# A chain of eight image layers: where GpSimd takes a norm's power in the first two stages

## The reference

```python
x = x + gate_conv(ln(x))       # stage 0: softmax gate over the 256 pixels
t = t + topk_ffn(ln(t))        # stage 1: FFN for the 127 best of 256 tokens of each image
x = x + deform_conv(ln(x))     # stage 2: deformable 3x3
t = t + moe_gelu(ln(t))        # stage 3: 8 experts
x = x + attention(ln(x))       # stage 4
t = t + moe_64(ln(t))          # stage 5: 8 experts
x = x + spectral_conv(ln(x))   # stage 6: 3x3 conv with weights w / sigma
t = t + moe_ln(ln(t))          # stage 7: 8 experts

def ln(v):                     # in every stage
    return (v - mean(v)) / sqrt(var(v) + eps)

def sigma(w, a, b, c):         # depends on the weights alone, complex numbers
    for _ in range(20):
        d = normalize(einsum('oihw,o,i,h->w', w, a*, b*, c*))
        c = normalize(einsum('oihw,o,i,w->h', w, a*, b*, d*))
        b = normalize(einsum('oihw,o,h,w->i', w, a*, c*, d*))
        a = normalize(einsum('oihw,i,h,w->o', w, b*, c*, d*))
    d = normalize(...)
    return abs(einsum('oihw,o,i,h,w->', w, a*, b*, c*, d*))
```

## Time and profile before

| | |
|---|---|
| median of 3 runs | 1166.83 us (1162.14, 1166.83, 1176.15) |
| the profiled execution | 1172.36 us, of which the span of instructions is 1170.6 us |
| mean granted TensorE clock in it | 0.850 of full speed |
| busy in the span | TensorE 81%, VectorE 60%, ScalarE 42%, GpSimd 38% |
| stage 0, stage 1 in the profile | about 27 to 135 us, about 138 to 240 us |

### The profile page before, as it was taken

How to read it: one execution, slowest core, us unless ns; L and a number is a source line. 1 busy time by engine, 2 the same in 40 slices (tenths; PEclk the granted TensorE clock), 3 DMA queues, 4 the chain that set the end, 5 groups by cost and what they waited for, 6 DMA issues and landing times.

```text
span 1170.6 us, 16680 instructions
## 1 busy us (share of the span) xinstructions
PE 951.9 (81%) x4266; PEld 567.0 (48%) x4266; DVE 697.0 (60%) x2439; ACT 493.2 (42%) x966; POOL 445.8 (38%) x1234
## 2 busy tenths in 40 slices
PE   2656387758998998989888777799988767999998
PEld 2545265435554555555534434465554554444443
DVE  2876676746455664554467756656675554566653
ACT  1322222245445654552445445333343012666664
POOL 4565566631543535446244221134564321111100
PEclk9999996659889988998789887857779666999999
DMA  4500000000000000000000000000000000000000
GB/s 74 86 0 1 0 1 0 0 1 1 1 1 0 0 0 0 1 1 1 1 0 1 0 0 1 1 0 0 0 1 0 1 0 0 5 5 4 9 5 9
DMA packets 26352, 6.21 MB, mean 5 GB/s; under 512 B 24068, under 2 KB 26244, under 8 KB 26308
## 3 DMA queue, kind: packets, MB, share of 16 engines
q1 hardware_dynamic: 26308, 5.70, 2.8%
HBM read 4.65 MB, written 1.05 MB: 5 GB/s over the span
## 4 chain that ended last, share of the span: by engine, by line
PE 44%; issue 16%; DVE 10%; POOL 5%; ACT 4%; DVEq 0%; POOLq 0%; ACTq 0%; another core or an unknown queue 0%
PE banks L1449 8%; PE banks L1275 6%; PE banks L1158 5%; PE banks L1159 3%; PE banks L1089 3%; PE banks L1466 2%; PE banks L1473 2%; PE banks L1267 2%; PE banks L1417 2%; DVE weighted L1994 1%; DVE summed L1998 1%; DVE V L1720 1%; PE banks L1263 1%; PE banks L1230 1%; POOL rstd L646 1%
## 5 line engine op out<-in xcount | busy, mean ns | idle before, releaser
L962 ACT ACTIVATE scratch<-banks,b 128x512 f32<-128x512 f32 x224 | 144.3, 683 | 57.2 <-PE banks L1159 45.1
L1449 PE MATMUL banks<-scratch,W 128*64 128x512 f32 (+1 forms) x448 | 151.8, 661 | 0.4
L1889 DVE TENSOR_TENSOR scratch<-banks,XR 128x1024 f32<-128x1024 f32 x72 | 87.5, 1224 | 87.3 <-PE banks L1267 61.1
L1158 PE MATMUL banks<-VS,W_hi 128*128 128x512 f32 x240 | 120.6, 503 | 2.1 <-DVE X L2067 1.0
L646 POOL TENSOR_TENSOR rstd<-vareps,neghalf 128x4 f32<-128x4 f32 x64 | 66.8, 1044 | 128.6 <-DVE vareps L1708 124.0
L1159 PE MATMUL banks<-VS,W_lo 128*128 128x512 f32 x240 | 106.4, 443 | 0.0
L1994 DVE SCALAR_TENSOR_TENSOR weighted<-banks,b,cwide 128x512 f32<-128x512 f32 x72 | 53.9, 748 | 73.7 <-PE banks L1449 72.9
L1275 PE MATMUL banks<-scratch,region 128*64 128x256 f32 x576 | 88.0, 432 | 3.0 <-DVE scratch L1889 3.0
L1720 DVE TENSOR_SCALAR V<-X,moments,rstd 128x64 f32 (+1 forms) x256 | 67.6, 328 | 36.7 <-POOL rstd L646 32.6
L973 ACT ACTIVATE cwide<-banks 128x512 f32<-128x512 f32 x96 | 57.4, 598 | 73.8 <-PE banks L1466 73.5
L1132 PE MATMUL banks<-ident,V 128*128 128x128 f32 x128 | 33.7, 354 | 58.5 <-DVE V L1720 58.4
(11 more groups left out here) (289 smaller groups left out, 2039.6 us busy)
## 6 DMA issues: line engine op xcount, KB each, us to landing
W<-in_L_ffn_W SPq DMA_DIRECT2D x3, 512.0 KB
X<-in_x SPq DMA_DIRECT2D x8, 128.0 KB, 2.7
out<-X SPq DMA_DIRECT2D x8, 128.0 KB, 2.0
cwide<-in_L_ffn_W SPq DMA_DIRECT2D x2, 256.0 KB
KC<-in_L_conv_kernel SPq DMA_DIRECT2D x2, 144.0 KB
W<-in_L_ffn_W SPq DMA_DIRECT2D x1, 256.0 KB
cwide<-in_L_ffn_w SPq DMA_DIRECT2D x2, 128.0 KB
Ko<-in_L_conv_w SPq DMA_DIRECT2D x1, 144.0 KB, 3.7
```

Source lines behind the costliest of these rows:

```text
L962: act.activation(hid[:, c % 4, :], bank[c % 2][:, :], ACT.Gelu, bias=b1[s][:, w:w + 1]).then_inc(h_ready, 1)
L1158: pe.matmul(out, hi, VS[u][:], start=True, stop=False)
L1449: ins = pe.matmul(y, W2[s][:, w, :], hid[:, c % 4, :], start=opens, stop=closes, skip_group_check=True)
L1889: vec.tensor_tensor(S[:, k % 3], pair(p), xr, ALU.mult).then_inc(s_ready, 1)
```

## The change

In `body`, which sets GpSimd's order, `seg1` now stands ahead of the norm's power (`prep`) in stages 0 and 1 too, as it did in stage 2. In stage 5 it stays where it was.

```diff
--- before.py
+++ after.py
@@ -662,7 +662,7 @@
                     step = None if s not in STEP0 else i * 2 + (STEP0[s] + u) if s == 2 else i + STEP0[s]
                     first_half = step is not None and (u == 0 or s == 2)
                     second_half = step is not None and (u == 1 or s == 2)
-                    if s == 2:
+                    if s == 2 or first_half and s < 2:
                         seg1(step)
                     if s in MOE and (u == 0 or not wrap):
                         powers(i * 2 + (MOE0[s] + u + 1), s)
@@ -670,7 +670,7 @@
                         prep(i * 2 + 2 - wrap, s_next)
                     elif not wrap:
                         prep(i * 2 + 3, s)
-                    if s != 2 and first_half:
+                    if s > 2 and first_half:
                         seg1(step)
                     if first_half:
                         seg2(step)
```

## The result

| | before | changed |
|---|---|---|
| median of 20 runs each | 1166.71 us | 1158.83 us |
| lowest to highest | 1158.55 to 1176.15 | 1151.97 to 1167.97 |
| profiled execution, span | 1170.6 us | 1164.1 us |
| mean granted TensorE clock in it | 0.850 | 0.847 |

The ratio, which leaves out runs over 1.5% above the fastest of their kernel, is 0.9936, 95% interval 0.9916 to 0.9956: 0.64% less time, 7.5 us (the two medians lie 7.9 us apart). The 20 runs of one kernel spread over 16 to 18 us, so the total alone says that the change helps, but not through what. The traces say that, since kernels with the same code up to a mark reach it at nearly the same time: stage 1 starts at 134.38 and 134.35 us in two kernels with the old order in stage 0, at 130.16, 130.18 and 130.55 in three with the new one.

The account below looks back on a forecast made before the run. It took a closed loop with GpSimd's power as a link to bound stage 0's and 1's trips; 0.5 + 3.0 + 0 + 3.3 + 0.4 = 7.2 us off the 1166.83 median gives 1159.6 us, range 1153 to 1167.

Parts of the forecast that it names:

- The closed loop: Stage 0's second trip: GpSimd, TensorE and VectorE wait for each other in a loop of 25.04 us, GpSimd's power being one link.
- Stage 0, trips two to four: `seg1` starts 1.01 us earlier per trip, where the power stood, covered by TensorE's 3.63 us idle: 3.0 us in all.
- The first trip: Stage 0: `T1` is ready at 35.79, so `seg1` starts at about 35.9 instead of 36.41, 0.5 us gained.
- Stage 1's first trip: TensorE is busy turning the block's output until 148.68, later than `bsq` at 148.00, so gain and price are both 0.
- Stage 1, trips two to four: The power's distance to `seg1` comes off each trip, covered by TensorE's idle time: 1.15 + 1.15 + 1.0 = 3.3 us.
- The 0.4 us for a faster `seg1`: Stage 1: VectorE stands still during part of `seg1`, which then runs 0.13 us faster a trip, 0.4 us in all.
- TensorE's cover in stage 1: TensorE's idle time of 1.56 us before `slot2` covers the earlier `seg1`, leaving 0.4 us.
- The sign of right and wrong: Profile sign at line 1108: TensorE's idle time in stage 1 would be 0.4 us instead of 1.56.
- The thin cover: Stage 1: with the power behind `seg1`, V is ready only 0.2 to 0.3 us before TensorE turns it.
- The late norm: Rival: TensorE waits for V in stage 1 instead, losing half that stage's gain, 1.7 us: 1161.3 us, chance 0.13.
- The later stages: Stages 2 to 7: nothing behind stage 1 changes its order, so they shift as they are.
- rivals of a better and a colder clock: TensorE's mean clock 0.01 higher, 1153.6 us, chance 0.13; or lower in stages 2 to 7, about 1166 to 1172, chance 0.12.

## Why the prediction was right

The forecast was 1159.6 us and 0.6% less; measured were 1158.83 and 0.64%. The mechanism was right; that the sum came out so near is in part luck, as two errors cancel. Its steps one by one:

**The closed loop** was right. GpSimd, TensorE and VectorE wait for each other in a ring, so a microsecond in it is a microsecond of the trip, although GpSimd is busy 38% of the span and has 5% of the chain. A second power cost 4.3 us in stage 0 ahead of `seg1` and 0.4 behind it, and taking the one behind away gave nothing more.

**Stage 0, trips two to four**, was sized 3.0 us and gave 4.22 - 0.64 = 3.58. The excess is 0.15 to 0.2 us a trip. `seg1` itself runs in 2.10 instead of 2.17 us; the rest is spread over several distances of 0.01 to 0.04 us. **The first trip**, bounded by `T1`, was sized 0.5 and gave 0.64.

**Stage 1's first trip**: forecast 0, measured -4.18 against -4.22, so 0.

**Stage 1, trips two to four**, was sized 3.3 us, with 0.4 us more for a faster `seg1`, and gave 6.94 - 4.18 = 2.76. **The 0.4 us for a faster `seg1`** had the wrong sign: it became slower by 0.08 to 0.17 us a trip. This is the one term that failed, and it explains most of what is missing: 0.4 us that did not come and 0.35 that were lost. The loops shrank by 25.86 - 24.83 and 25.83 - 24.80, that is 1.03 us each, where 1.15 + 0.13 was forecast. The excess of stage 0 (0.7 us with its first trip) and the lack of stage 1 (0.9 us) cancel, so the sum is better than its parts.

**TensorE's cover in stage 1** was read too simply. The prediction took the idle time of 1.56 us for a fixed cover and expected 0.4 us to be left. In the changed kernel it is 2.48, 2.63 and 0.76 us in the three trips, by the level of TensorE's clock. Where the matmuls were slow, 0.52 us was left, so the sum of the prediction is right for that level. The sign of right and wrong that it derived from it was not one.

**The thin cover** was right in size: 0.2 to 0.3 us forecast, 0.33 measured. The late norm took nothing. It begins at once behind that: a second power makes TensorE wait 0.75 us. The norm of line 1720 was expected to wait for `rstd` in eight places. VectorE idles in front of it in seven: in stage 0's first trip it comes just after the power's end (39.73 against 39.37) and doesn't wait.

**The later stages** shift as they are. Span less stage 2's start is 930.3 us before and 930.7 after. In the other kernels with the same code there it ranges from 926.1 to 938.9, with mean granted clocks of 0.825 to 0.864. That is nearly as wide as the spread between runs of one program, and the reason that no single total here settles a few microseconds. The clock alone doesn't order it: the longest stretch, 938.9 us, has 0.852. As to the rivals of a better and a colder clock, the mean granted clock of the changed kernel's 20 runs has a median of 0.848. In three other sets of runs of the kernel before the median is 0.837, 0.844 and 0.851. So no shift is seen that is larger than the one between sets; a small one is not excluded.

## What to carry to other kernels

When engines hand work round a ring, look at which of them is last to come at each hand-over, and take off its list whatever the next one doesn't need: 1 us of work was free behind the next hand-over and cost 1 us a trip where it stood. Then read how much room the moved work has until somebody wants it (here 2 us in one stage and 0.33 in the other), and what runs beside the moved piece at its new time, not at its old one. After such a move ask for the next late arrival: copies that stand behind long work without need (`msum` behind four exponentials, `T1` behind the last one) gave nearly as much again, 6.2 us.

## What the runs showed of the hardware that I had not expected

**GpSimd beside VectorE.** Two products of 64 x 18 elements take 0.39 us with VectorE idle, 0.58 in the kernel before in stage 1 and 0.74 beside VectorE's comparisons (0.88 in stage 1's first trip). All of `seg1` up to `bsq` takes 2.10 to 3.47 us by what VectorE does meanwhile. A busy VectorE is not enough: in stage 0 the products take 0.39 us although VectorE works on line 1796, which reads one of its inputs from `banks`.

**The granted clock that the early rows print isn't the pace.** In the kernel before, the view of windows (busy time and count of TensorE, its weight loads, VectorE, ScalarE and GpSimd, then the granted clock and the DMA's share and rate) says 1.00 for 156 to 163 us and 0.50 for 207 to 214 us, the same part of two trips:

```profile
156.00:163.00 7.00, 5.05 (x17) 2.88 (x17) 6.49 (x31) 1.09 (x3) 5.45 (x11) 1.00 0.01 2
...
207.00:214.00 7.00, 5.05 (x18) 3.15 (x18) 6.57 (x34) 0.88 (x2) 5.16 (x13) 0.50 0.00 0
```

Yet the same four matmuls of 512 columns take the same time in both, and little more than half of it at 181 us:

```profile
156.16 1.98 PE L1208 MATMUL banks<-scratch,W2b 128*64 128x512 f32 x4
...
181.39 1.08 PE L1208 MATMUL banks<-scratch,W2b 128*64 128x512 f32 x4
...
207.85 1.98 PE L1208 MATMUL banks<-scratch,W2b 128*64 128x512 f32 x4
```

So the engine ran at 1.2 GHz in that part of stage 1's first trip, although the column reads as 2.4 there; for the early stages the durations have to be read. The mean of 0.850 is thereby too high, and not by the same amount in every kernel: between 165 and 172 us the column says 1.00 in the kernel before, where the four matmuls take 1.98 us, and 0.52 in the changed one.
